# A ring of four buffers for the shared expert's outputs, and the first four tile loads ahead of the last four stores

## The reference

```python
x = hidden_states.reshape(-1, D)                    # 2048 tokens, D = 256
topk_idx, tw = _route(x, router_w, bias)            # 4 of 16 experts for each token
combine = (jax.nn.one_hot(topk_idx, E, dtype=tw.dtype) * tw[..., None]).sum(1)
h = jnp.einsum('td,edf->etf', x, gate_w)
u = jnp.einsum('td,edf->etf', x, up_w)
y = jnp.einsum('etf,efd->etd', jax.nn.silu(h) * u, down_w)
routed = jnp.einsum('etd,te->td', y, combine)
sh = jax.nn.silu(x @ sh_gate_w) * (x @ sh_up_w) @ sh_down_w    # the shared expert, for every token
return (routed + sh).reshape(hidden_states.shape)
```

## Time and profile before

| what | value |
|---|---|
| median of 3 runs | 930.06 us (929.49 to 932.44) |
| time of the profiled execution | 932.86 us |
| its span, first to last instruction | 931.0 us |
| PE busy | 853.7 us, 92% of the span |
| DVE busy | 557.0 us, 60% |
| POOL busy | 454.2 us, 49% |
| ACT busy | 439.5 us, 47% |
| DMA | mean 122 GB/s |

### The profile page before, as it was taken

The page is one execution under the profiler, slowest core; times in us unless marked ns, Lnnn a source line. Parts: engine busy times, 40 slices in busy tenths (PEclk is TensorE's granted clock), DMA queues, the critical chain, the costliest instruction groups (busy, mean ns, idle before and its releaser), DMA issues.

```text
span 931.0 us, 20120 instructions
## 1 busy us (share of the span) xinstructions
PE 853.7 (92%) x5868; PEld 612.2 (66%) x5869; DVE 557.0 (60%) x1640; ACT 439.5 (47%) x1159; POOL 454.2 (49%) x609
## 2 busy tenths in 40 slices
PE   6989599988998999998999988996999999999995
PEld 2666489865886888887787765554555555556553
DVE  3788538848126889888887898574333333333325
ACT  2466355444425777777777864210223232323224
POOL 4988411102125455533555444777654544445445
PEclk9999989997899999999999999998999999999998
DMA  9610111000029999990511100755555555555547
GB/s 311 206 44 6 34 30 39 26 12 12 24 71 306 282 296 333 269 273 32 212 36 37 36 25 35 273 207 170 132 93 83 91 84 88 87 89 87 88 62 255
DMA packets 86642, 113.50 MB, mean 122 GB/s; under 512 B 8224, under 2 KB 77600, under 8 KB 86048
## 3 DMA queue, kind: packets, MB, share of 16 engines
q1 hardware_dynamic: 71392, 90.49, 32.6%
q0 software_dynamic: 14448, 19.34, 12.7%
q10 hardware_dynamic: 720, 2.63, 0.8%
HBM read 48.40 MB, written 64.05 MB: 121 GB/s over the span
## 4 chain that ended last, share of the span: by engine, by line
PE 73%; DVE 9%; ACT 5%; issue 5%; DMA 4%; POOL 3%; SPq 0%; DVEq 0%; ACTq 0%; POOLq 0%
PE bank L1044 48%; PE bank L1057 7%; PE bank L1520 6%; PE bank L1493 3%; PE bank L1530 3%; DMA ys<-xs 1%; DVE arena L2434 1%; DMA const<-in_const 1%; DVE arena L2025 1%; DMA arena<-ys 1%; POOL arena L894 1%; DMA ys<-arena 1%; PE bank L1388 1%; PE bank L1230 1%; PE bank L1036 1%
## 5 line engine op out<-in xcount | busy, mean ns | idle before, releaser
L1044 PE MATMUL bank<-arena 128*128 (+6 forms) x1344 | 424.9, 456 | 21.1 <-ACT arena L1681 8.6
L1044 PEld LDWEIGHTS bank<-arena 128*128 128x128 f32 (+1 forms) x1344 | 231.3, 191 | 136.2 <-issue 96.9
L1004 POOL DMA_INDIRECT ys<-arena x79 | 123.1, 1558 | 117.8 <-DVE arena L2548 104.2
L2540 DVE SCALAR_TENSOR_TENSOR arena<-arena,bank 128x256 f32<-128x256 f32 x79 | 38.0, 481 | 144.9 <-ACT arena L1927 144.9
L1927 ACT ACTIVATE arena<-bank 128x256 f32<-128x256 f32 x79 | 30.4, 384 | 173.1 <-PE bank L1044 173.1
L1057 PEld LDWEIGHTS bank<-const,arena 128*128 128x128 f32 x572 | 69.6, 142 | 63.9 <-issue 57.7
L2434 DVE TENSOR_REDUCE arena<-bank 128x4 f32<-128x512 f32 x128 | 86.9, 679 | 23.8 <-PE bank L1493 12.1
L853 POOL TENSOR_TENSOR lr<-mv,const 128x1 f32<-128x1 f32 x48 | 9.1, 190 | 188.0 <-DVE mv L1976 188.0
L1057 PE MATMUL bank<-const,arena 128*128 128x128 f32 x572 | 93.8, 277 | 5.0 <-DVE arena L2044 1.7
L1887 ACT ACTIVATE arena<-arena 128x512 f32<-128x512 f32 x116 | 74.0, 638 | 38.1 <-DVE arena L2440 37.1
L1520 PE MATMUL bank<-const,arena 128*128 128x128 f32 x512 | 79.7, 278 | 4.3 <-ACT arena L1894 3.4
(11 more groups left out here) (287 smaller groups left out, 1334.7 us busy)
## 6 DMA issues: line engine op xcount, KB each, us to landing
grid<-arena SPq DMA_DIRECT2D x1, 37264.0 KB, 134.3
arena<-in_f_w SPq DMA_DIRECT2D x18, 768.0 KB, 7.1
arena<-grid SPq DMA_DIRECT2D x79, 137.0 KB, 2.7
arena<-ys SPq DMA_DIRECT2D x8, 512.0 KB, 7.2
inT<-in_ctxT SPq DMA_DIRECT2D x30, 128.0 KB, 2.0
X<-in_x SPq DMA_DIRECT2D x1, 2048.0 KB
arena<-in_c_w SPq DMA_DIRECT2D x2, 1024.0 KB, 5.0
ys<-arena SPq DMA_DIRECT2D x1, 2048.0 KB, 10.4
```

What stands on the lines that cost most here:

```text
L1004: pool.indirect_dma_start(ys, bass.IndirectOffsetOnAxis(ap=number, axis=0), s_y[t.ring(YR)], None, compute_op=ALU.add).then_inc(l_sy[t.rin ...
L1044: m = pe.matmul(o, lhs[k], rhs[k], start=k == 0, stop=k == n - 1)
L2540: dve.scalar_tensor_tensor(out=f_a[0][:, t.p * EF:(t.p + 1) * EF], in0=f_h[t.p], scalar=s_w[t.p], in1=bank[2 + t.p][:, EF:2 * EF], op0=ALU ...
```

## The change

The outputs of the shared expert get a ring of four buffers, `h_out`: the two `xs`, and the last two of the four buffers `s_y`, which the slots use only later. y(b) now waits for the store of b-4. There is a semaphore for each of the four. The first two slots that write into the two borrowed buffers wait for the last stores from there, and POOL's first `q_scatter_` waits for all four semaphores. SP issues the loads of slots 0 to 3 before the stores of batches 8 to 11, and no longer waits for up(11) ahead of them; slots 4 to 7 follow the stores. To have two semaphores free, two others of the start of the kernel (`a_tab`, `f_filled`) are merged into `a_ready`, with the counts 8 and 2 in place of 6 and 1.

```diff
+HR = 4
+        h_out = [xs[0][:], xs[1][:]] + s_y[YR - HR + 2:]
-        l_hs = [sem("l_hs0"), sem("l_hs1")]
+        l_hs = [sem(f"l_hs{i}") for i in range(HR)]
...
-            sp.wait_ge(f_filled, 1)
+            sp.wait_ge(a_ready, 2)
...
-                sp.dma_start(shared_rows[b, 0], xs[b % 2][:]).then_inc(l_hs[b % 2], 16)
+                sp.dma_start(shared_rows[b, 0], h_out[b % HR]).then_inc(l_hs[b % HR], 16)
...
-            for b in range(GB, DONE - 2):
+            for b in range(GB, DONE - GB):
                 store_shared(b)
             sp.wait_ge(f_routed, 5)
             for i in range(3):
                 sp.wait_ge(l_sc[i], 64 * ((HB + 2 - i) // 3))
+            for i in range(SR // 2):
+                load_slot(Slot(i, i, 0))
+            for b in range(DONE - GB, DONE):
+                store_shared(b)
             wait(sp, h_up, turn(DONE - 1), 1)
-            for i in range(SR):
+            for i in range(SR // 2, SR):
                 load_slot(Slot(i, i, 0))
-            for b in range(DONE - 2, DONE):
-                store_shared(b)
...
-                    pool.wait_ge(a_tab, 6)
+                    pool.wait_ge(a_ready, 8)
...
-            for i in range(2):
-                pool.wait_ge(l_hs[i], 16 * (DONE // 2))
+            for i in range(HR):
+                pool.wait_ge(l_hs[i], 16 * (DONE // HR))
...
-                if t.b >= 2:
-                    dve.wait_ge(l_hs[t.p], 16 * t.half)
-                dve.tensor_tensor(xs[t.p][:], bank[(2, 7)[t.p]][:, 0:D], X[:, t.b, 0:D], ALU.add).then_inc(h_yc.sem, 1)
+                if t.b >= HR:
+                    dve.wait_ge(l_hs[t.b % HR], 16 * (t.b // HR))
+                dve.tensor_tensor(h_out[t.b % HR], bank[(2, 7)[t.p]][:, 0:D], X[:, t.b, 0:D], ALU.add).then_inc(h_yc.sem, 1)
...
                 if not t.peeled or t.b >= YR:
                     dve.wait_ge(l_sy[t.ring(YR)], 16 * t.lap(YR))
+                elif t.b >= YR - HR + 2:
+                    dve.wait_ge(l_hs[t.b - YR + HR], 16 * (DONE // HR))
```

More of the change, by code:

```diff
@@ L540, in build @@
         t_add, t_bns, t_var, t_pow, t_neg, t_out = (sem(f"t_{name}") for name in ("add", "bns", "var", "pow", "neg", "out"))
-        a_tab = sem("a_tab")
         copied = step("copied", 1)
@@ L649, in build @@
         d_y = step("d_y", 1)
-        f_filled = sem("f_filled")
         f_tp = step("f_tp", 1)
@@ L1993, in _ @@
             m.then_inc(a_ready, 1)
-            dve.memset(f_fill, 0.0).then_inc(f_filled, 1)
+            dve.memset(f_fill, 0.0).then_inc(a_ready, 1)
             dve.wait_ge(l_rows, 32)
@@ L1998, in _ @@
                 sl = slice(i * D, (i + 1) * D)
-                dve.tensor_tensor(a_cos[:, sl], c("cos"), row(gain), ALU.mult).then_inc(a_tab, 1)
+                dve.tensor_tensor(a_cos[:, sl], c("cos"), row(gain), ALU.mult).then_inc(a_ready, 1)
                 pairs = lambda v: v.rearrange("p (n two) -> p n two", two=2)
@@ L2002, in _ @@
                     dve.tensor_tensor(pairs(a_sin[:, sl])[:, :, z], pairs(c("sin"))[:, :, z],
-                                      pairs(row(gain))[:, :, 1 - z], ALU.mult).then_inc(a_tab, 1)
+                                      pairs(row(gain))[:, :, 1 - z], ALU.mult).then_inc(a_ready, 1)
             dve.wait_ge(l_const, 16)
-            dve.wait_ge(a_tab, 6)
+            dve.wait_ge(a_ready, 8)
             def a_qkb_(t):
```

## The result

The changed kernel took 929.02 us (median of 20 runs) against 932.07 us for the one before (20 runs on the same chips). The ratio is 0.9972, with a 95% interval of 0.9962 to 0.9982, that is 2.6 us less (1.7 to 3.5). The forecast was 2.8 us less. As a time it was 927.3 us, 1.7 us too low: it started from 930.06 us, the median of the first 3 runs, and the median of 20 is 932.07. In a second comparison, together with the first experiments, it came out at 0.9962 (0.9943 to 0.9980), 3.5 us less. Its profiled execution took 928.88 us, with a span of 927.1 us.

What follows compares the result with a forecast made beforehand. PE bounds the kernel, so only its idle or slow time counts. The 7.6 us shift, cut to 4.5 us by POOL at slot 8, less 1.7 us of clock, gives 2.8 us less: 927.3 us from 930.06, range 924.5 to 929.5.

Steps and rivals of the forecast that it cites:

- the shift: Before the first slots: PE gets 7.6 us ahead of its old times.
- POOL's cap at slot 8: Slot 8's load waits for POOL's unmoved slot 0 scatter, leaving 4.5 us of the 7.6 us.
- y(6), y(7) and the downs: Shared expert's end: store waits go, down(8) starts 4.7 us earlier at 633.65, downs end 6.4 us earlier, 1.7 of it clock.
- The first slots: First slot's transpose: its tile is there at 639.5, before PE at 640.6, so the 1.24 us wait vanishes.
- POOL: POOL's stream before the slots: 64 grid scatters stay back to back, so slot 0's scatter stays at 661.75.
- the play of 1.1 us: End of POOL's grid scatters: up to 1.1 us earlier or some 0.5 us later; no change taken.
- The stop: Before slot 8: PE arrives at 665.4 and stands 3.1 us for its tile, until 668.5.
- The price of the stop: After the stop at slot 8: the lower clock costs 1.7 us, with ends of 0 and 3.4 us.
- Whether the clock falls: At slot 8: 3.1 us of idling lies between 2.1 and 6.16 us, both followed by 0.50, so the clock falls.
- The sum: Whole kernel: 4.5 us left at slot 8 less 1.7 us for the clock gives 2.8 us less.
- the clock stays down longer: Rival, after the stop at slot 8: low clock up to twice as long, saving 1.1 us, 929.0 us; 18%.

Runs made afterwards that it cites:

- the undisturbed kernel: The changed kernel with POOL's scatters of slots 0 to 5 each ahead of one of the last six grid scatters: ratio 0.9920 against before.
- The ring of three: The changed kernel with three output buffers (`HR = 3`) in place of four, run twice: ratios 0.9958 and 0.9956 against the kernel before.

## Why the prediction came out right

The total was right, 2.8 us for a measured 2.6, and so was the mechanism: the shift, POOL's cap at slot 8, the stop and the lower clock behind it. That the total fits to 0.2 us is luck, as the steps on the price and the sum show. By its steps:

- *y(6), y(7) and the downs.* The downs were forecast 23.0 us behind the routing row (633.65 less 610.61), measured +23.1. PE's idle time was to be 1.4 us and was 1.47, at a granted clock of 1.00. They take 7.17 us at the upper level where I had 6.9, so the 8.58 us of before held 1.4 us of the lower clock and not 1.7. Right, with 0.3 us too much for the clock.
- *The first slots.* The first transpose was forecast at +30.0 and stands at +30.1, with no wait for its tile. Right.
- *POOL.* The scatter of slot 0 was to stay at +51.1; it came at +50.25 and +50.15, inside the play of 1.1 us that I gave it. The grid scatter that took 2.04 us before has no like after the change; the longest in this stretch beside L2525 took 1.07 us. In all other profiles with POOL's old order the scatter starts between +49.6 and +50.3 as well, or waits for DVE, so the profile of before was the odd one.
- *The stop.* Forecast 3.1 us, measured 2.61 and 2.15. PE got to slot 8 at +54.8, as forecast. POOL's scatter came 0.9 and 1.0 us earlier than forecast, and in the first profile the tile came 0.4 us later behind it. Right in kind, a little large.
- *The price of the stop.* This is the mis-sized term. I took 1.7 us (1.4 by the length of the downs above). From the stop at slot 8 to the group with slot 12 the changed kernel needs 3.5 us more than the undisturbed kernel in one profile, 2.5 us more in the other. The lower clock holds for 6.7 us in one and 3.3 us in the other, which is 3.3 or 1.7 us lost; the remaining 0.2 to 0.8 us go with PE's slow restart (it idles another 0.31 and 0.73 us behind the transposes of slot 8), which the prediction had not.
- *Whether the clock falls.* I took one row for it, the 2.1 us of idling before 50 us. All fourteen profiles have the same gap there, 2.16 to 2.17 us long and ended by ACT. In five of them the clock fell behind it, and in nine it stayed at 1.00. The first profile of the changed kernel is one of the nine, as its stretch shows:

```profile
51.60:53.60 2.00, 2.00 (x14) 1.90 (x15) 1.55 (x7) 0.33 (x1) 1.72 (x4) 1.00 0.00 0
```

  So the row that I argued from was a chance of that execution. At slot 8 the clock fell behind all four stops of over 2 us (2.02, 2.15, 2.61 and 4.05). That is what the forecast said, on thinner evidence than it seemed.
- *The sum.* At slot 8 the changed kernel is 5.0 us ahead of the profile of before in one profile and 5.5 in the other, not 4.5, and pays 3.5 or 2.5 us, not 1.7: 1.5 or 3.0 us at slot 12. The 2.6 us of the first comparison lie between, the 3.5 us of the second a little above. Two errors, both of the size of a microsecond, had opposite signs. And the yardstick was itself one of several: against the two other profiles of the old schedule (slot 12 at +75.2 and +75.3) the same two profiles win 2.1 to 3.6 us. My rival "the clock stays down longer" is thus not a rival but the other half of the same case, and the forecast's chance should have gone to the two together.

The Trainium skill, "TensorE: Matmul & The Clock Gate", section "HAM oscillation — how this bites in real kernels", tells of a kernel in which each DMA wait between bursts of matmuls, of some 3 to 5 us, sends the clock down. Here that held at the four stops of 2.02 to 4.05 us at slot 8, and not at the one of 0.49 us. The prediction said that the trace of before agrees at both places; it shows the fall at both, but neither was a DMA wait: the gap before 50 us ended with ACT, and the 6.16 us with DVE. On the Trainium skill's "SBUF — State Buffer", section "Who interferes with whom", the case stays open: the grid scatter at 631.49 ran beside L2525 in its normal 0.96 us, which speaks for that section and against my reading of the 2.04 us, but scatters beside the list operations took 1.2 to 1.5 us before and after the change.

## What to carry to other kernels

Before adding buffers to a ring, look at what stands in front of the store in its DMA queue: here 2.3 MB of weights did, and putting two stores ahead of them was worth as much as two more buffers. When a stage is to start earlier, list every queue that must be ready when it does, and subtract: POOL had 4.5 us of slack at slot 8, the shift was 7.6 us, and only reordering POOL brought in the rest. A short new stop of the bottleneck engine costs more than its length: behind stops of 2.15 and 2.61 us PE lost another 2.5 and 3.5 us. By the profiles a shift that ends in a stop can so be worth less than a smaller one that just fits: slot 12 comes at 70.4 with the weights behind two stores, and at 71.7 and 73.1 in the changed kernel. The times don't separate the two.

## What the runs showed of the hardware

- The same two gaps before and after the first transposes (1.2 to 1.5 and 0.8 to 0.9 us, with 0.4 us of work between) left the clock at 1.00 in the profile of the kernel before and in two others with the old order of the loads, and sent it to 0.50 in three more. I had read "1.24 us is harmless" from one profile.
- One and the same gap can be followed by either level: the 2.17 us before 50 us, above, by 0.50 in five profiles and by 1.00 in nine.
- The length of the low stretch differs too. At slot 8 it was some 3.4 us behind 2.02 and 2.15 us of idling and 6.7 us behind 2.61 and 4.05 us, which leaves open whether the stop decides it. The ring of three has the same wait in both of its profiles, 5.20 and 5.18 us before the downs, and there the clock stood at 0.50 for some 3.4 us in one and 6.7 us in the other; in the second it fell while PE still idled, and the downs took 9.13 us, not 8.84. So the length of the wait alone does not set it.
- Behind the transposes of slot 8, where PE had waited for the DMA, it idled once more, 0.31 to 0.73 us, with nothing to wait for in the profile: behind the stop of only 0.49 us it was 0.68 us. Its sequencer was reading the expert's number from SBUF then, as the list of the instructions of line L1604 in that profile has it between 664.9 and 666 us (shortest, median and longest ns of one, first and last start):

```profile
L1604 PEldq TENSOR_LOAD <-arena x1: 458/458/458, 665.2 to 665.2; - x1
```

  In the running stage this read (0.3 to 0.7 us between 640 and 720 us of the changed kernel) lies beside the matmuls before it. That the read is what PE idles for fits these rows and was not tried.
- DVE's wait at y(6) for the store of batch 4, the same three weight loads in front of it, was 7.23 us in one profile and 5.1 to 5.4 us in three others. By the row that ends it, the store landed at about +20.9 in the first and at +18.7 to +19.1 in the three. A single profile is good for the chain, and not for the size of a wait on a busy DMA queue.
